# Half of the first early tile's matmuls moved among the last token tiles, with the order around them laid out anew

## The chip, the cores and the metric

The kernel runs on one core of one Trainium2 chip. The metric is the device time in microseconds of one execution. Three timed runs of the kernel before gave 883.22, 883.50 and 887.41 us (median 883.5).

## The reference, cut to what matters

```python
x = x + ffn(cond(x, cond_weights, itok), W_gate, b_gate, W_e, b_e)     # x: 64 x 64 x 1024, f32

cond:  W = weights[condition]                      # one 64 x 64 matrix of 16 for each batch entry
       y = einsum('bct,bcd->bdt', x, W)            # 4096 tokens of 1024 features
ffn:   logits = y @ W_gate + b_gate                # 8 experts
       _, top_idx = top_k(logits, 2)
       y_all = relu(einsum('bsd,edh->bseh', y, W_e) + b_e)
       out = mean of the two chosen experts' rows
```

So there are 8192 (token, expert) pairs, and each needs a row of 1024 times the expert's 1024 x 1024 matrix.

## The kernel before, in words

**Token stage.** The 4096 tokens are taken in 32 tiles of 128 (n = 0 to 31). For a tile, TensorE multiplies the tile of x by a block-diagonal matrix (`product`, L548) into one of two accumulators psO0 and psO1. ScalarE copies it to SBUF (`y_out`, L700) and writes it to `y_rows` in HBM (L703). VectorE transposes the copy (`turn_tokens`, L855). For every group g of four tiles there follows a chain that finds out which experts each token goes to: TensorE `gate` in two halves (L560), ScalarE copies the logits (L709), TensorE `unstack` (L580, L581), VectorE `choose` (L882 to L890), TensorE `ranks` (L587 to L593), VectorE `slots` (L895 to L928), TensorE `fill` (L572), VectorE `list_out` (L935 to L938). Then SyncE writes the lists to a table in HBM (`table_out`, L325). Dictionaries such as `GATE`, `RANKS` and `FILL` say after which tile each step stands on its engine. Product n+2 may not start before `y_out(n)`, because there are two accumulators.

**Split weights.** The expert product is done in three parts (high x high, low x high, high x low), so each chunk of 128 weight rows is split in two: ScalarE makes `w_hi`, VectorE the rest `w_lo`. Expert 0's eight chunks are split during the token stage (`split_first`).

**Early tiles.** Seven tiles of expert 0 (t = 0 to 6) need only the first entries of the table and are begun before the whole table is known. For each of them SyncE reads the list (`read_first`, L311), VectorE makes addresses (`read_from`, L972), GpSimd gathers the rows (L451), VectorE transposes them (`turn_early`, L1009), ScalarE takes the high part (`early_hi`, L730), VectorE the low part (`early_lo`, L1014), TensorE does 48 matmuls of 512 columns (`early_products`, L607: 8 chunks k, three parts, two halves of the columns), VectorE adds the bias (`finish_early`, L993), ScalarE applies relu (L724), and GpSimd adds the rows to the output. Steps of the last token groups stand between the matmuls of early tiles 0 and 1 as `hooks`.

**Main stage.** `schedule` (L942 to L966) works out which expert each tile has; the table is read back (ScalarE, L770) and turned into addresses (VectorE, L1081 to L1091). Then tile after tile is gathered (L465), transposed (L1020), split (L736, L1031), multiplied (L607), finished and added to the output. The weights of expert 1 and on are loaded by SyncE in chunks (L334) and split by ScalarE (L719) and VectorE (L875). With these inputs expert 0 has nine tiles (0 to 8), and tile 9 is the first of expert 1. 69 tiles are multiplied in all.

**What sets the order.** Each engine runs its program in the order written, and waits on semaphores. VectorE holds, in its order, `turn_rows(8)` and `finish_early(6)` behind the splitting of expert 1's first four chunks (`ahead(EARLY)`), and `early_lo(8)` behind those. SyncE's program goes, after the token tiles: stores and copies of x to the output (L305, L340; each `copy` is 1 MB and waits for the copy before the last), between them the last three `table_out`, then the rest of the copies, and only then the weights of expert 1:

```python
table_out(NG - 1)
read_first(6)
for c in range(6, len(left)):
    copy(c)
sp.wait_ge(s_alo, EARLY)
sp.wait_ge(s_bias, 16)
load_bias(1)
```

## Time and profile before

| what | value |
|---|---|
| timed runs | 883.22, 883.50, 887.41 us, median 883.5 |
| profiled execution, its own time | 886.42 us |
| its span (first to last instruction) | 884.7 us |
| mean granted TensorE clock | 0.984 |
| TensorE busy | 851.7 us (96%) |
| VectorE, ScalarE, GpSimd busy | 422.4, 256.5, 449.9 us |
| `L607` matmuls | 3 x 1104 records, 341.7 + 340.6 + 340.4 us |

The profiled execution took 886.42 us, 1.7 us more than its span, and 2.9 us more than the median of the timed runs. A record of the profile holds one of two levels of TensorE's clock: 1.0 stands for 2.4 GHz and 0.5 for 1.2 GHz, and a mean over a stretch lies between.

### The profile page before, as it was taken

The page shows a single profiled execution, that of the slowest core. Times are in us where ns is not written, and L with a number is a line of the kernel's source. Part 1 is how long each engine was busy: PE and PEld are TensorE (multiplying, and loading weights), DVE is VectorE, ACT ScalarE, POOL GpSimd, SP SyncE. Part 2 cuts the span into 40 slices and gives each one's busy share as a digit, 9 for nine tenths or more (in the row PEclk, how much of TensorE's full clock was granted, in tenths as well). Part 3 has the DMA queues.
Part 4 walks back from the last instruction along what each step waited for, and adds up shares of the span by engine and source line. Part 5 has one row for each costly group of instructions (what it writes and reads, how often), then busy time and mean ns, then how long its engine had stood idle before and what let it go on. Part 6 is the DMA issues. An engine that isn't in the chain of part 4 may idle for free.

```text
span 884.7 us, 16708 instructions
## 1 busy us (share of the span) xinstructions
PE 851.7 (96%) x4154; PEld 674.4 (76%) x4155; DVE 422.4 (48%) x595; ACT 256.5 (29%) x310; POOL 449.9 (51%) x500
## 2 busy tenths in 40 slices
PE   7898899999999999999999999999999999999993
PEld 4354478888888888888888888888888888888882
DVE  6697866836643273335533363336333733333320
ACT  5564512134421251114211331115111511112220
POOL 3002325366467667654665556555755565555311
PEclk9898999999999999999999999999999999999997
DMA  9999798998955695447754595547654664444433
GB/s 337 418 417 348 265 333 275 329 346 245 290 125 107 127 294 120 99 95 202 198 106 90 101 294 108 109 96 211 172 115 95 189 122 104 91 100 99 79 48 47
DMA packets 51034, 162.47 MB, mean 184 GB/s; under 512 B 11594, under 2 KB 11658, under 8 KB 50986
## 3 DMA queue, kind: packets, MB, share of 16 engines
q0 software_dynamic: 24544, 76.74, 40.3%
q1 hardware_dynamic: 20618, 67.79, 20.9%
q10 hardware_dynamic: 5840, 17.57, 5.1%
q8 instruction: 14, 0.23, 0.1%
q14 instruction: 18, 0.15, 0.0%
HBM read 106.74 MB, written 70.52 MB: 200 GB/s over the span
## 4 chain that ended last, share of the span: by engine, by line
PE 88%; DMA 4%; DVE 4%; issue 1%; ACT 1%; SPq 1%; POOL 0%; ACTq 0%; DVEq 0%; POOLq 0%
PE psO L607 85%; PE psO L548 2%; DMA y_rows<-ys 1%; DVE turned L855 1%; DMA first<-slot_table 1%; DMA slot_table<-lists 1%; DMA raw<-in_L_cond_weights 1%; ACT ys L700 1%; PE psG L560 1%; DVE w_lo L868 0%; SPq L325 0%; DVE place_hot L910 0%; DVE run_hot L918 0%; DVE idx_all L885 0%; POOL out L494 0%
## 5 line engine op out<-in xcount | busy, mean ns | idle before, releaser
L607 PE MATMUL psO<-w_hi,a_hi 128*128 (+1 forms) x1104 | 341.7, 391 | 0.2
L607 PE MATMUL psO<-w_lo,a_hi 128*128 (+1 forms) x1104 | 340.6, 390 | 0.0
L607 PE MATMUL psO<-w_hi,a_lo 128*128 (+1 forms) x1104 | 340.4, 389 | 0.0
L465 POOL DMA_INDIRECT rows<-y_rows,idx_g x248 | 260.6, 1051 | 106.7 <-issue 52.7
L607 PEld LDWEIGHTS psO<-w_hi,a_lo 128*128 128x128 f32 x1104 | 207.6, 188 | 43.3
L607 PEld LDWEIGHTS psO<-w_lo,a_hi 128*128 128x128 f32 x1104 | 207.7, 188 | 43.2
L607 PEld LDWEIGHTS psO<-w_hi,a_hi 128*128 128x128 f32 x1104 | 206.7, 188 | 44.4 <-issue 1.8
L1031 DVE TENSOR_TENSOR a_lo<-ys,a_hi 128x1024 fp32r<-128x1024 f32 x62 | 75.9, 1224 | 113.8 <-ACT a_hi L736 113.8
L724 ACT ACTIVATE ys<-ys 128x1024 f32<-128x1024 f32 x33 | 35.0, 1061 | 259.5 <-DVE ys L993 259.5
L724 ACT ACTIVATE rows<-rows 128x1024 f32<-128x1024 f32 x33 | 35.0, 1060 | 253.9 <-DVE rows L993 253.9
L993 DVE TENSOR_TENSOR ys<-psO,bias 128x1024 f32<-128x1024 f32 x33 | 40.3, 1222 | 125.4 <-PE psO L607 98.9
L993 DVE TENSOR_TENSOR rows<-psO,bias 128x1024 f32<-128x1024 f32 x33 | 40.4, 1225 | 119.2 <-PE psO L607 89.1
L875 DVE TENSOR_TENSOR w_lo<-raw,w_hi 128x1024 f32 x56 | 65.3, 1223 | 36.9 <-ACT w_hi L719 36.9
L1020 DVE STREAM_TRANSPOSE ys<-rows 128x1024 f32<-128x1024 f32 x62 | 76.8, 1238 | 9.6 <-DMA rows<-y_rows,idx_g 9.6
L494 POOL DMA_INDIRECT out<-rows,idx_s x31 | 55.9, 1802 | 39.9 <-issue 16.4
L494 POOL DMA_INDIRECT out<-ys,idx_s x31 | 52.1, 1682 | 38.6 <-ACT ys L724 17.7
L461 POOL COPY idx_g<-idx_all 128x4 uint32 x62 | 25.9, 418 | 86.9 <-issue 54.5
L736 ACT CAST a_hi<-ys 128x1024 fp32r<-128x1024 f32 x62 | 65.0, 1048 | 10.3 <-issue 10.2
L451 POOL DMA_INDIRECT raw<-y_rows,from_q x28 | 30.4, 1086 | 65.2 <-DVE bias L1009 35.1
L719 ACT CAST w_hi<-raw 128x1024 f32 x56 | 54.9, 1048 | 7.4 <-DMA raw<-in_L_ffn_W_e 6.2
L855 DVE STREAM_TRANSPOSE turned<-ys 128x1024 f32<-128x1024 f32 x32 | 39.5, 1240 | 14.5 <-ACT ys L700 12.4
L700 ACT COPY ys<-psO 128x1024 f32<-128x1024 f32 x32 | 32.4, 1012 | 23.1 <-PE psO L548 20.1
(141 smaller groups left out, 331.4 us busy)
## 6 DMA issues: line engine op xcount, KB each, us to landing
raw<-in_L_ffn_W_e SPq DMA_DIRECT2D x56, 512.0 KB, 6.0
y_rows<-ys ACTq DMA_DIRECT2D x32, 512.0 KB, 8.3
out<-in_x SPq DMA_DIRECT2D x14, 1024.0 KB, 9.7
rows<-in_x SPq DMA_DIRECT2D x16, 512.0 KB, 11.8
more_x<-in_x SPq DMA_DIRECT2D x16, 512.0 KB, 11.1
bias<-in_L_ffn_b_e SPq DMA_DIRECT2D x8, 512.0 KB
rows<-y_rows,idx_g POOLq DMA_INDIRECT x248
raw<-in_L_ffn_W_e POOLq DMA_DIRECT2D x4, 512.0 KB, 8.7
```

What stands on the lines that cost most here:

```text
L465: pool.indirect_dma_start(out=rows[:, slot, a * DQ:(a + 1) * DQ], out_offset=None, in_=y_parts[0:(1 + TOK) * Q, :], in_offset=bass.Indirec ...
L494: pool.indirect_dma_start(out=out, out_offset=bass.IndirectOffsetOnAxis(ap=idx_s[:, m:m + 1], axis=0), in_=o_sb[m], in_offset=None, comput ...
L607: last = nc.tensor.matmul(ps[:, h * BANK:(h + 1) * BANK], a[:, p, k * P:(k + 1) * P], w[:, bass.ds(slot + (k * H + h * BANK), BANK)], star ...
L700: nc.scalar.copy(ys[:, s, :].rearrange("p (q k j) -> p q k j", q=Q, k=KD), psO[n % 2][:, :].rearrange("p (k q j) -> p q k j", q=Q, k=KD)). ...
L719: nc.scalar.copy(w_hi[:, bass.ds(at, H)], raw[:, k, :]).then_inc(s_hi, 1)
L724: nc.scalar.activation(out_of(t), out_of(t), ACTF.Relu, scale=0.5).then_inc(s_out, 1)
L736: nc.scalar.copy(a_hi[:, m % 2, :], ys[:, m % 2, :]).then_inc(s_ahi, 1)
L855: V.transpose(turned[:, g % 2, :, s * R:(s + 1) * R], ys[:, s, :].rearrange("p (b i) -> p b i", i=R)).then_inc(s_turn, 1)
L875: V.tensor_tensor(w_lo[:, bass.ds(at, H)], raw[:, k, :], w_hi[:, bass.ds(at, H)], ALU.subtract).then_inc(s_split, 1)
L993: V.tensor_tensor(out_of(t), psO[m % 2][:, :], bias[:, bass.ds((e % 2) * H, H)], ALU.add).then_inc(s_bo, 1)
L1020: V.transpose(ys[:, p, :].rearrange("p (k a i) -> p k a i", k=KD, a=Q), rows[:, p, :].rearrange("p (a k j) -> p k a j", k=KD, a=Q)).then_i ...
L1031: V.tensor_tensor(a_lo[:, p, :], ys[:, p, :], a_hi[:, p, :], ALU.subtract).then_inc(s_alo, 1)
```

## The change: what it does

Early tile 0 no longer shares a buffer with the later ones: its transposed rows stand in a new buffer `early_f`. Its left 512 columns are multiplied in `psX`, a bank that is free by then (`ahead`, 24 matmuls), in six pieces behind token tiles 26 to 31. Its right 512 columns are multiplied in psO0 after the token tiles (`early_products(0, ..., hs=(1,))`). For that, `turn_early(0)` moves from behind tile 28 to behind tile 24, and ScalarE's `early_hi(0)` with it; `early_lo(0)` stands behind tile 25. Early tile 1 is turned behind tile 30 and tile 2 before `list_out(NG - 2)`. On VectorE, `choose` now stands ahead of `turn_tokens` and `read_from` behind it. The hooks are spread over early tiles 0, 1 and 2 in another order, and `fill(NG - 3)` has become one. In the middle stretch the table's addresses are made before `finish_early(3)`, `turn_early(5)` and `early_lo(5)`, and ScalarE issues the table's read before `early_hi(4)`.

```diff
@@ -106 @@
+            early_f = lend("early_f", [P, D])
@@ -250 @@
-        FILL = {G * g + 11: g for g in range(NG - 2)}
+        FILL = {G * g + 11: g for g in range(NG - 3)}
+        AHEAD = {26: [0], 27: [1, 2], 28: [3], 29: [4], 30: [5], 31: [6, 7]}
@@ products @@
-                                for h in range(NH):
+                                for h in hs:
                                     last = nc.tensor.matmul(
-                                        ps[:, h * BANK:(h + 1) * BANK], a[:, p, k * P:(k + 1) * P],
+                                        psX[:, :] if h in apart else ps[:, h * BANK:(h + 1) * BANK], a[:, p, k * P:(k + 1) * P],
...
+                def ahead(ks):
+                    if ks[0] == 0:
+                        pe.wait_ge(s_alo, 1)
+                        pe.wait_ge(s_split, RAW)
+                    products(tile(0, 0), None, 0, 0, ks, hs=(0,), apart=(0,))
...
+                    if n in AHEAD:
+                        ahead(AHEAD[n])
-                early_products(0, hooks={3: lambda: ranks(NG - 2), 4: lambda: gate(NG - 1, 1, 0),
-                                         5: lambda: gate(NG - 1, 1, 1), 7: lambda: unstack(NG - 1)})
-                early_products(1, hooks={0: lambda: fill(NG - 2), 2: lambda: ranks(NG - 1), 7: lambda: fill(NG - 1)})
-                early_products(2)
+                early_products(0, hooks={2: lambda: fill(NG - 3), 5: lambda: ranks(NG - 2),
+                                         7: lambda: gate(NG - 1, 1, 0)}, hs=(1,))
+                early_products(1, hooks={0: lambda: gate(NG - 1, 1, 1), 2: lambda: unstack(NG - 1),
+                                         5: lambda: fill(NG - 2), 7: lambda: ranks(NG - 1)})
+                early_products(2, hooks={4: lambda: fill(NG - 1)})
@@ scalar @@
-                    if n == NTILE - 4:
+                    if n == NTILE - 8:
                         early_hi(0)
-                early_hi(1)
+                    if n == NTILE - 2:
+                        early_hi(1)
                 logits_out(NG - 1)
...
-                early_hi(4)
-                relu(tile(0, 2))
                 for g in range(NG):
                     act.wait_ge(s_sc[g], LAND)
...
+                early_hi(4)
+                relu(tile(0, 2))
@@ vector, finish_early @@
-                    finish(tile(0, t), 0)
+                    if t:
+                        finish(tile(0, t), 0)
+                    else:
+                        dve.wait_ge(s_bias, 16)
+                        dve.wait_ge(s_mm, 1)
+                        own(V.tensor_tensor(o_first[:, 0, 0:BANK], psX[:, :], bias[:, 0:BANK], ALU.add))
+                        V.tensor_tensor(o_first[:, 0, BANK:H], psO[0][:, BANK:H], bias[:, BANK:H], ALU.add).then_inc(s_bo, 1)
@@ vector, the token tiles @@
-                    if n == NTILE - 3:
-                        early_lo(0)
-                    if n in FROM:
-                        read_from(FROM[n])
                     if n in UNSTACK:
                         choose(UNSTACK[n])
                     turn_tokens(n)
+                    if n in FROM:
+                        read_from(FROM[n])
+                    if n == NTILE - 7:
+                        early_lo(0)
...
-                    if n == NTILE - 4:
+                    if n == NTILE - 8:
                         turn_early(0)
+                    if n == NTILE - 2:
+                        turn_early(1)
+                    if n == NTILE - 1:
+                        early_lo(1)
                 list_out(NG - 3)
                 slots(NG - 2)
-                turn_early(1)
-                early_lo(1)
+                finish_early(0)
                 choose(NG - 1)
+                turn_early(2)
                 list_out(NG - 2)
-                finish_early(0)
+                early_lo(2)
                 slots(NG - 1)
                 read_from(4)
-                turn_early(2)
-                early_lo(2)
+                finish_early(1)
                 list_out(NG - 1)
-                finish_early(1)
...
                 schedule()
-                early_out(4, EARLY)
-                finish_early(3)
-                turn_early(5)
-                early_lo(5)
...
+                finish_early(3)
+                turn_early(5)
+                early_lo(5)
+                early_out(4, EARLY)
                 finish_early(4)
```

VectorE around token tiles 22 to 25. `turned<-ys` is `turn_tokens`, `from_q` is `read_from`, `w_lo` is `split_first`, `lists` is `list_out`, and `MAX` and `MAX_INDEX` are `choose`. Before:

```order
L855 STREAM_TRANSPOSE turned<-ys 128x32x32
L972 TENSOR_SCALAR from_q<-first,part_q 128x4
L882 MAX idx_all<-psR 128x8 x3
L883 MAX idx_all<-psR 128x8
L885 MAX_INDEX idx_all<-idx_all,psR 128x8 x3
L886 MAX_INDEX idx_all<-idx_all,psR 128x8
L887 TENSOR_TENSOR idx_all<-idx_all 128x64
L890 TENSOR_TENSOR mask<-idx_all 128x32
L855 STREAM_TRANSPOSE turned<-ys 128x32x32
L868 TENSOR_TENSOR w_lo<-bias,w_hi 128x1024
L855 STREAM_TRANSPOSE turned<-ys 128x32x32
L935 CAST lists<-psL 64x64
```

The same place in the changed kernel, from `choose` on, to the low part of early tile 0:

```order
L898 TENSOR_TENSOR idx_all<-idx_all 128x64
L901 TENSOR_TENSOR mask<-idx_all 128x32
L866 STREAM_TRANSPOSE turned<-ys 128x32x32
L983 TENSOR_SCALAR from_q<-first,part_q 128x4
L879 TENSOR_TENSOR w_lo<-bias,w_hi 128x1024
L866 STREAM_TRANSPOSE turned<-ys 128x32x32
L946 CAST lists<-psL 64x64
L1026 STREAM_TRANSPOSE early_f<-raw 128x1024
L866 STREAM_TRANSPOSE turned<-ys 128x32x32
L1031 TENSOR_TENSOR a_lo<-early_f,a_hi 128x1024
```

`from_q` has moved behind `choose` and the transpose, and the turn of early tile 0 and its low part stand on either side of tile 25's transpose. The same exchange of `from_q` and `choose` is made at tiles 19, 27 and 31.

TensorE from token tile 26 to tile 28. `psG` is `gate`, `psR` `unstack`, `psL` `fill`. Before:

```order
L548 MATMUL psO<-rows,raw 128x512 x2
L560 MATMUL psG<-turned,wgb 32x128 x16
L548 MATMUL psO<-rows,raw 128x512 x2
L580 MATMUL psR<-stack,LT 128x32
L581 MATMUL psR<-raw 128x32
L572 MATMUL psL<-place_hot,run_hot 64x64 x8
L548 MATMUL psO<-more_x,raw 128x512 x4
```

And in the changed kernel:

```order
L550 MATMUL psO<-rows,raw 128x512 x2
L562 MATMUL psG<-turned,wgb 32x128 x16
L609 MATMUL psX<-w_hi,a_hi 128x512
L609 MATMUL psX<-w_lo,a_hi 128x512
L609 MATMUL psX<-w_hi,a_lo 128x512
L550 MATMUL psO<-rows,raw 128x512 x2
L582 MATMUL psR<-stack,LT 128x32
L583 MATMUL psR<-raw 128x32
L574 MATMUL psL<-place_hot,run_hot 64x64 x8
```

The first chunk's three matmuls into `psX` stand between the gate of tile 26 and the product of tile 27, so whatever they wait for the product of tile 27 waits for too.

VectorE in the middle stretch, where the table becomes addresses (`idx_all`, `idx_row`). Before, the finish of tile 3 (`ys<-psO`), the turn and low part of tile 5 stand ahead of it:

```order
L987 SCALAR_TENSOR_TENSOR first_to<-first_f,behind 128x3
L993 TENSOR_TENSOR ys<-psO,bias 128x1024
L1009 STREAM_TRANSPOSE bias<-raw 128x1024
L1014 TENSOR_TENSOR a_lo<-bias,a_hi 128x1024
L1081 COPY ys<-ys 128x1024
L1083 STREAM_TRANSPOSE ys<-ys 128x8x4x32
L1085 TENSOR_SCALAR idx_all<-ys,part_q 128x1024
L1091 CAST ys<-ys 32x256 x4
```

And in the changed kernel:

```order
L1096 COPY ys<-ys 128x1024
L1098 STREAM_TRANSPOSE ys<-ys 128x8x4x32
L1100 TENSOR_SCALAR idx_all<-ys,part_q 128x1024
L1106 CAST ys<-ys 32x256 x4
L997 TENSOR_SCALAR ys<-ys,empty_to 128x256
L998 SCALAR_TENSOR_TENSOR idx_row<-ys 128x256
L1004 TENSOR_TENSOR ys<-psO,bias 128x1024
L1026 STREAM_TRANSPOSE bias<-raw 128x1024
L1031 TENSOR_TENSOR a_lo<-bias,a_hi 128x1024
```

The three instructions of early tiles 3 and 5 have moved behind the whole address block.

## Rows read from the trace of the kernel before

**Rows 1.** The page, busy time of each engine (share of the span) and instructions.

```profile
PE 851.7 (96%) x4154; PEld 674.4 (76%) x4155; DVE 422.4 (48%) x595; ACT 256.5 (29%) x310; POOL 449.9 (51%) x500
```

**Rows 2.** Windows: busy time of five engines, then granted clock, DMA share, GB/s.

```profile
75.00:85.00 10.00, 8.85 (x79) 4.71 (x76) 9.15 (x19) 2.20 (x6) 3.49 (x3) 0.66 0.83 308
...
110.00:120.00 10.00, 8.17 (x48) 6.21 (x52) 7.57 (x32) 0.00 (x0) 0.49 (x1) 0.83 1.02 389
...
140.00:200.00 60.00, 60.00 (x266) 49.66 (x265) 36.30 (x61) 14.77 (x14) 31.97 (x31) 1.00 1.02 328
```

**Rows 3.** Timeline, TensorE, tile 22: start, us, line, idle before it and releaser.

```profile
74.77 0.23 PE L587 MATMUL psR<-mask,raw 128*128 128x24 bf16 x3 [1.96 <-DVEq L891]
...
76.27 2.07 PE L560 MATMUL psG<-turned,wgb 128*32 128x128 f32 x32 [1.15 <-DVE turned L855]
78.27 3.78 PE L548 MATMUL psO<-more_x,raw 128*128 128x512 f32 x4
```

**Rows 4.** Timeline of TensorE, token tiles 26 to 31 and early tile 0.

```profile
90.57 1.98 PE L548 MATMUL psO<-rows,raw 128*128 128x512 f32 x4
...
93.49 1.98 PE L548 MATMUL psO<-rows,raw 128*128 128x512 f32 x4
...
106.97 1.96 PE L548 MATMUL psO<-more_x,raw 128*128 128x512 f32 x4 [0.92 <-ACT ys L700]
...
111.83 0.44 PE L572 MATMUL psL<-place_hot,run_hot 128*64 128x64 f16 x8 [2.00 <-DVEq L921]
...
117.11 0.62 PE L607 MATMUL psO<-w_lo,a_hi 128*128 128x512 f32 x2
117.56 0.61 PE L607 MATMUL psO<-w_hi,a_lo 128*128 128x512 f32 x2
```

**Rows 5.** Timeline of VectorE: read_from(0), tile 24, slots(4), tile 26, early tile 0.

```profile
72.69 0.23 DVE L972 TENSOR_SCALAR from_q<-first,part_q 128x4 uint32<-128x4 uint32 x1 [2.30 <-DMA first<-slot_table]
...
89.56 1.23 DVE L855 STREAM_TRANSPOSE turned<-ys 128x1024 f32<-128x1024 f32 x1
...
92.28 0.18 DVE L895 TENSOR_TENSOR idx_all<-idx_all,psR 128x64 f32<-128x64 f32 x1
...
96.21 1.25 DVE L855 STREAM_TRANSPOSE turned<-ys 128x1024 f32<-128x1024 f32 x1
...
103.59 1.25 DVE L1009 STREAM_TRANSPOSE bias<-raw 128x1024 f32<-128x1024 f32 x1 [0.21 <-DVE lists L938]
```

**Rows 6.** Timeline of ScalarE: high part of early tile 0.

```profile
104.87 1.04 ACT L730 CAST a_hi<-bias 128x1024 fp32r<-128x1024 f32 x1 [4.90 <-DVE bias L1009]
```

**Rows 7.** Timeline of VectorE: last list, schedule, then the address block.

```profile
139.86 0.21 DVE L938 TENSOR_TENSOR lists<-list_high,psL 64x64 uint32<-64x64 f32 x1
...
154.55 0.16 DVE L942 TENSOR_SCALAR raw<-raw 1x8 f32<-1x8 f32 x1
...
160.59 0.17 DVE L978 CAST parted<-first 128x12 f32<-128x12 uint32 x1
...
167.43 1.07 DVE L1081 COPY ys<-ys 128x1024 uint32<-128x1024 uint32 x1
...
173.34 0.47 DVE L987 SCALAR_TENSOR_TENSOR idx_row<-ys 128x256 uint32<-128x256 f32 x1
```

**Rows 8.** Timeline of GpSimd: the copy that opens the gather of tile 7.

```profile
172.23 0.32 POOL L461 COPY idx_g<-idx_all 128x4 uint32 x1 [6.19 <-issue]
```

**Rows 9.** Timeline of SyncE DMA issues: last eight copies, expert 1 weights.

```profile
147.79 29.81 SPq L340 DMA_DIRECT2D out<-in_x  x8
...
179.31 19.57 SPq L334 DMA_DIRECT2D raw<-in_L_ffn_W_e  x7
```

**Rows 10.** Timeline of VectorE: fourth split of expert 1, low part of tile 8.

```profile
198.97 1.23 DVE L875 TENSOR_TENSOR w_lo<-raw,w_hi 128x1024 f32 x1 [0.45 <-ACT w_hi L719]
...
204.53 1.23 DVE L1031 TENSOR_TENSOR a_lo<-ys,a_hi 128x1024 fp32r<-128x1024 f32 x1 [2.06 <-ACT a_hi L736]
```

**Rows 11.** The chain of waits where tile 8 starts: start, us, what.

```profile
206.17 0.08 issue
```

More of the change, by code:

```diff
@@ L594, in ranks, with products @@
                     last.then_inc(s_rank, 1)
-                def products(t, ps, e, slot, ks=range(KD), hooks={}):
+                def products(t, ps, e, slot, ks=range(KD), hooks={}, hs=range(NH), apart=()):
                     n, half, m = t
@@ L611, in products, with early_products @@
                                         stop=(k == KD - 1 and a is a_lo))
-                    if ks[-1] == KD - 1:
+                    if hs[-1] == NH - 1:
                         last.then_inc(s_mm, 1)
-                def early_products(t, ks=range(KD), hooks={}):
+                def early_products(t, hooks={}, hs=range(NH)):
+                    pe.wait_ge(s_alo, t + 1)
+                    if t >= 2:
+                        pe.wait_ge(s_bo, t - 1)
+                    else:
+                        pe.wait_ge(s_yc, NTILE - 1 + t)
+                    products(tile(0, t), psO[t % 2], 0, 0, hooks=hooks, hs=hs)
+                def ahead(ks):
                     if ks[0] == 0:
-                        pe.wait_ge(s_alo, t + 1)
+                        pe.wait_ge(s_alo, 1)
                         pe.wait_ge(s_split, RAW)
-                        if t >= 2:
-                            pe.wait_ge(s_bo, t - 1)
-                        else:
-                            pe.wait_ge(s_yc, NTILE - 1 + t)
-                    products(tile(0, t), psO[t % 2], 0, 0, ks, hooks)
+                    products(tile(0, 0), None, 0, 0, ks, hs=(0,), apart=(0,))
                 def all_products(t):
@@ L729, in early_hi @@
                         act.wait_ge(s_mm, t - 1)
-                    nc.scalar.copy(a_hi[:, t % 2, :], early_t).then_inc(s_ahi, 1)
+                    nc.scalar.copy(a_hi[:, t % 2, :], early_t if t else early_f[:, :]).then_inc(s_ahi, 1)
                 def parts(t):
@@ L1000, in finish_early @@
                         dve.wait_ge(s_yout[t % OS], 16 * NG)
-                    finish(tile(0, t), 0)
+                    if t:
+                        finish(tile(0, t), 0)
+                    else:
+                        dve.wait_ge(s_bias, 16)
+                        dve.wait_ge(s_mm, 1)
+                        own(V.tensor_tensor(o_first[:, 0, 0:BANK], psX[:, :], bias[:, 0:BANK], ALU.add))
+                        V.tensor_tensor(o_first[:, 0, BANK:H], psO[0][:, BANK:H], bias[:, BANK:H], ALU.add).then_inc(s_bo, 1)
                 def turn_early(t):
                     dve.wait_ge(s_yx[t % 2], (t // 2 + 1) * (Q * 16))
-                    if t:
+                    if t == 1:
+                        dve.wait_ge(s_split, KD)
+                    if t > 1:
                         dve.wait_ge(s_alo, t)
-                    else:
-                        dve.wait_ge(s_split, KD)
-                    V.transpose(early_t.rearrange("p (k a i) -> p k a i", k=KD, a=Q),
+                    V.transpose((early_t if t else early_f[:, :]).rearrange("p (k a i) -> p k a i", k=KD, a=Q),
                                 fetched[t % 2].rearrange("p (a k j) -> p k a j", k=KD, a=Q)).then_inc(s_zt, 1)
@@ L1013, in early_lo @@
                     dve.wait_ge(s_ahi, t + 1)
-                    V.tensor_tensor(a_lo[:, t % 2, :], early_t, a_hi[:, t % 2, :], ALU.subtract).then_inc(s_alo, 1)
+                    V.tensor_tensor(a_lo[:, t % 2, :], early_t if t else early_f[:, :], a_hi[:, t % 2, :], ALU.subtract).then_inc(s_alo, 1)
                 def turn_rows(t):
```

## The prediction

> **What bounds the kernel now.** The page says that TensorE is busy for 96% of the span [rows 1], and the chain of waits goes along its matmuls from 112 us to 871 us almost without a gap. Two matmul pairs of full clock start 0.455 us apart [rows 4], so one matmul costs 0.2275 us and a tile (48 of them) 10.92 us. The reader should take two things from this. Time can be won only where TensorE waits or runs at the low clock, which is before 112 us. And what is won there stays won only if nothing behind it comes due at a fixed time. So I read the timelines of the token stage first, then the DMA share of the stretch behind it, then the waits of tiles 2 to 8.
>
> In the token stage TensorE waits 1.96 us at tile 21 for `choose`, which stood on VectorE behind a `read_from` that waited 2.30 us for its list [rows 3, 5]. Then the work of tile 22 runs at about half speed. The windows give the length of the low clock: 0.34 / 0.5 x 10 us = 6.8 us in 75 to 85 us, and 0.17 / 0.5 x 10 = 3.4 us in 110 to 120 us [rows 2]. At half speed each costs half its length, 3.4 and 1.7 us. At the end TensorE waits 0.92 us for a copy and 2.00 us for `fill(5)` [rows 4].
>
> Behind it, the DMA engines are full: share 1.02 from 140 to 200 us [rows 2]. The last eight copies are issued over 29.81 us from 147.79, and expert 1's weights from 179.31 on [rows 9]. VectorE splits the fourth chunk at 198.97, and the low part of tile 8, which stands behind that, starts at 204.53 and lasts 1.23 [rows 10]. Tile 8 starts at 206.25, after a break of 0.08 us in the chain [rows 11]. So tile 8 has its operand 205.76, only 0.4 us before TensorE comes free. This is the second bound, and it hangs on the DMA queue, not on TensorE.
>
> **The change part by part.** All of it is a schedule by hand, from durations of rows.
>
> *`choose` ahead of `read_from` at tile 19.* Its wait for the list now stands behind the work that TensorE needs. `choose` (1.8 us: from behind `read_from` at 72.69 + 0.3 to `ranks` at 74.77) and the transpose (1.2, as of tile 24) begin at 70.4 us, when the transpose of tile 18 ends. TensorE's gate can start at 73.4 instead of 76.27, and tile 22's product at 74.4 instead of 78.27 [rows 3, 5]. With so short a wait I take the low clock there to be gone. VectorE becomes the limit for `fill(3)` (its `slots(3)`, 3.9 us as from 92.28 to 96.21, ends at 81.4 [rows 5]), and product 26 starts at about 86.7 instead of 90.57 [rows 4]: 3.9 us sooner.
>
> *`turn_early(0)` behind tile 24.* It starts when VectorE has done tile 24 and list 3. That was 91.1 us (89.56 + 1.17 + 0.39) and is now 88.6 [rows 5]. ScalarE has copied tile 24 from 83.5 on and is then held by `early_hi(0)`, which can start 1.28 us after the turn (104.87 against 103.59 before [rows 5, 6]), at 89.9. Copy 25 follows at 90.95, its transpose at 92.0, `early_lo(0)` at 93.2, and it lands at 94.4. TensorE stands at chunk 0 from 89.5: a wait of 4.9 us. Behind it is queued product 27, now at 95.1 instead of 93.49 [rows 4]. What tile 19 gave is spent, and 1.6 us more.
>
> *24 matmuls among tiles 26 to 31*: 24 x 0.2275 = 5.46 us. Beside them go the waits of 0.92 and of VectorE's transposes. Product 31 comes at 109.5 instead of 106.97, 2.5 us later [rows 4].
>
> *Behind tile 31.* `fill(5)` is no longer waited for (2.00 us), the low clock of 3.4 us need not come (1.7 us), and tile 0 has only 5.46 us left. Tile 1 starts at 121.4 instead of 111.83 + 0.37 + 10.92 + 1.7 + 3.8 of hooks = 128.6. That is 7.2 us, of which 1.1 us are hooks that still have to come. A wait of 0.4 us for the low part of tile 3 leaves 5.6 us at tile 3, on these sums 145.3 against 150.9.
>
> *The middle stretch.* The schedule takes 6.05 us (154.55 to 160.59) and the address block 6.6 (167.43 to 174.0) [rows 7]. Before, tile 5's turn stood between them. Now both stand ahead of it: VectorE comes to the schedule at 152.7 and to `finish_early(3)` at 165.3, the turn of tile 5 at 166.5, its low part lands at 170.0, and TensorE has finished tile 4 at 167.1. A new wait of 2.9 us is queued ahead of all of tile 5. It leaves 2.7 us at tile 7. In exchange the gather of tile 7, opened at 172.23 [rows 8], is opened at about 165, which nobody waits for.
>
> *Tile 8.* `list_out(6)` and the last list (139.86 before [rows 7]) come at 129.5 and 139.6, so SyncE's copies start when they did. Only the gap between the last copy (177.6) and the first weight load (179.31) can close, by up to 1.1 us, since tile 6's low part is ready 2 us sooner. Against that, the gathers of tiles 7 and 8 (1 MB) now stand among the copies in a full DMA stretch; before they stood beside the weight loads, so total bytes ahead of the fourth chunk are equal. I bound it by 1.1 us sooner and by 2.5 us later (a 1 MB copy takes 29.81 / 8 = 3.7 us, and the gathers move fewer bytes), and take 0.6 sooner, near the row's gap. The arrival of TensorE (203.5) no longer matters, and tile 8 starts at 205.6 instead of 206.25.
>
> The Trainium skill has a rule on this (DMA: Bandwidth & Descriptors, "Queues, rings and completion order"): each engine takes turns between the queues that have work, a packet at a time. By that rule the earlier gathers slow the copies on SyncE's queue and the weights start later, the upper bound. No row here separates the queues.
>
> *The sum.* On the profiled execution, 886.42 - 0.6 = 885.8. But it lies 2.9 us above the median of the runs shown, and the low clock at 112 us (1.7) is probably part of that difference: a median run has less for the change to take. And the wait of 4.9 us may bring low clock of its own: 3.4 us of it puts VectorE's lists and with them tile 8 later by 0.7, 6.8 us by 2.4 to 3.0. I take 1.1 for both. 883.5 - 0.6 + 1.1 = **884.0 us**, no change that can be told.
>
> **The rivals.** *A: the gain gets through.* If the DMA queue gives way when asked sooner, so that tile 8 follows TensorE's arrival, 2.7 us are left: 880.8. If tile 5's wait is not there either, 5.6 us: 877.9. For it: the gate before expert 1's weights (a semaphore of tile 6) comes 2 us sooner. Against: share 1.02 over 60 us [rows 2]. *B: the wait at tile 26 turns the clock down.* Before tile 22 TensorE had been idle for 1.96 and 1.15 us and the clock was low for 6.8 us [rows 2, 3]. A wait of 4.9 us is longer. Then products 27 to 29 run at half speed, every list comes 2.4 to 3.3 us later, the copies and the weights with them, and tile 8 too, 883.5 + 3 = 886.5. It goes over to slower by over 0.5% only together with C (2.5 us): 889. It decides when the low stretch starts before product 28. The Trainium skill says the same of waits inside a stream of matmuls (TensorE: Matmul & The Clock Gate, "HAM oscillation — how this bites in real kernels"); by that rule the clock does fall at tile 27. *C: the earlier gathers push the weights back* by up to 2.5 us, with the clock as it was: 886. For it: full DMA; against: equal bytes. *D: the change does not do what it says*: the matmuls ahead only move waits, because VectorE is the limit, and tile 1 starts near 126. The sums put it at 121.4; and since tile 8 is bound elsewhere, D ends at the forecast's time too.
>
> **How the numbers follow.** Forecast 0.50; A 0.20, of which half reaches the larger gain; B 0.17; C 0.13, and of B and C together a third lies with both. This kernel can tell 0.5% (4.4 us) from no change. Faster than 879.1: 0.10, with 0.01 for what I don't see. Slower than 887.9: 0.10, same reason. The range that should hold 8 in 10 goes from A's first value, 880.5, to B with a part of C, 888.
>
> **What would show it.** Right: product 22 near 74.4 at full clock; a TensorE wait of 4 to 5 us ahead of the first `psX` matmul; tile 1 some 7 us sooner; a wait of 2 to 3 us at tile 5; copies and weight loads at the same times as before, and a wait of 1 to 2 us at tile 8 for its low part. Wrong: expert 1's weights issued before 176 us, no wait at tile 5, or tile 8 started before 203; or the last list later than 142 us.

## The result, and the profile after

| what | before | changed |
|---|---|---|
| timed runs, same chip | 885.45 us median (883.22 to 890.86, 4 runs) | 895.03 us median (894.86 to 896.33, 4 runs) |
| ratio to before | | 1.0101, 95% interval 1.0081 to 1.0121 |
| profiled execution, its span | 886.42, 884.7 us | 895.16, 893.4 us |
| mean granted TensorE clock | 0.984 | 0.985 |

The change made the kernel slower by 1%, 9.6 us. The forecast was 884.0 us, and the range ended at 888.

The page of the changed kernel, its first section, against [rows 1]:

```profile
PE 852.7 (95%) x4154; PEld 674.2 (75%) x4155; DVE 422.5 (47%) x596; ACT 256.7 (29%) x310; POOL 447.1 (50%) x500
```

TensorE is busy for 1 us more in a span 8.7 us longer. The mean clock is the same. So the loss is mostly waiting. The windows say where, with the columns of [rows 2]:

```profile
75.00:85.00 10.00, 8.56 (x56) 4.15 (x56) 8.82 (x32) 4.69 (x10) 3.88 (x4) 0.86 1.02 371
...
110.00:120.00 10.00, 9.79 (x58) 6.96 (x59) 7.72 (x26) 3.24 (x4) 1.70 (x2) 1.00 0.79 280
140.00:200.00 60.00, 52.43 (x227) 42.04 (x226) 34.59 (x66) 10.44 (x10) 29.22 (x29) 0.94 0.92 295
```

From 140 to 200 us TensorE was busy without a break before; now 7.6 us of it are empty, its clock is 0.94, and the DMA share fell from 1.02 to 0.92. The token stage is better than before: at a higher clock from 75 us on (0.86 for 0.66), and with less idle time from 110 us on. The timeline of TensorE: its places that answer to [rows 3, 4], the last `fill`, and every wait over 1 us behind token tile 31:

```profile
74.78 1.98 PE L550 MATMUL psO<-more_x,raw 128*128 128x512 f32 x4
...
88.68 1.98 PE L550 MATMUL psO<-rows,raw 128*128 128x512 f32 x4
...
94.42 0.50 PE L609 MATMUL psX<-w_hi,a_hi 128*128 128x512 f32 x1 [1.19 <-DVE a_lo L1031]
...
95.22 1.88 PE L550 MATMUL psO<-rows,raw 128*128 128x512 f32 x4
...
111.42 1.88 PE L550 MATMUL psO<-more_x,raw 128*128 128x512 f32 x4
...
124.96 0.73 PE L609 MATMUL psO<-w_hi,a_hi 128*128 128x512 f32 x2
...
139.22 0.73 PE L609 MATMUL psO<-w_hi,a_hi 128*128 128x512 f32 x2 [1.46 <-DVE a_lo L1031]
...
144.88 0.44 PE L574 MATMUL psL<-place_hot,run_hot 128*64 128x64 f16 x8
...
151.26 0.73 PE L609 MATMUL psO<-w_hi,a_hi 128*128 128x512 f32 x2 [0.28 <-DVE a_lo L1031]
...
180.90 1.22 PE L609 MATMUL psO<-w_hi,a_hi 128*128 128x512 f32 x2 [6.92 <-DVE a_lo L1031]
```

The rows are products 22, 26, 27 and 31, and the starts of early tiles 1, 2, 3 and 5. Tile 1 starts 3.8 us sooner than before (128.77). Tile 3 starts when it did (151.61): 1.46 us went at tile 2, and more of the hooks stand behind tile 1's start. Tile 5 waits 6.92 us, and starts at 180.90 instead of 173.37; its first matmuls take 1.22 us a pair instead of 0.73, the lower clock of 1.2 GHz. Tile 8 follows at 215.39 instead of 206.25, without a wait. So in this trace the loss is made at tile 5: 7.5 us of later start, and 1.85 us of low clock behind it (tile 6 begins at 193.63, 12.73 us after tile 5, where a tile takes 10.88 at full clock). Nothing is gained or lost after tile 8 beyond half a microsecond.

The chain of waits of the changed kernel shows what stood ahead of tile 5. It is followed back to the end of the token stage (start, us, what), with most of its pieces left out:

```profile
118.69 13.57 DMA bias<-in_L_ffn_b_e
132.46 0.70 DVE more_x L1017
...
135.58 1.26 DVE bias L1026
136.86 1.06 ACT a_hi L740
137.94 1.23 DVE a_lo L1031
...
153.27 4.47 DMA slot_table<-lists
...
159.85 9.63 DMA ys<-slot_table
169.51 1.09 DVE ys L1096
...
177.25 1.25 DVE bias L1026
178.51 1.05 ACT a_hi L740
179.59 1.27 DVE a_lo L1031
180.90 34.20 PE psO L609 x142
```

At its head stands a transfer that the prediction never named: the 512 KB load of the bias, issued behind the stores and the first copies. VectorE's timeline shows who waits for it, the last list, which answers to [rows 7], and the wait for the high part of early tile 4:

```profile
132.46 0.69 DVE L1017 TENSOR_TENSOR more_x<-psX,bias 128x512 f32<-128x512 f32 x1 [8.84 <-DMA bias<-in_L_ffn_b_e]
...
133.79 0.31 DVE L893 MAX8 idx_all<-psR 128x8 f32<-128x8 f32 x3
...
145.36 0.22 DVE L948 TENSOR_SCALAR list_high<-psL 64x64 f32<-64x64 f32 x1 [0.97 <-issue]
145.61 0.21 DVE L949 TENSOR_TENSOR lists<-list_high,psL 64x64 uint32<-64x64 f32 x1
...
161.52 1.23 DVE L1031 TENSOR_TENSOR a_lo<-bias,a_hi 128x1024 fp32r<-128x1024 f32 x1 [4.82 <-ACT a_hi L740]
```

L1017 is `finish_early(0)`. It waits 8.84 us, and the last `choose` (the MAX8 row), the turn of tile 2, the list of group 6, `slots` and the last list stand behind it. The last list comes at 145.61 instead of 139.86; just before it VectorE idles for 0.97 us, until the `fill` that TensorE starts at 144.88 has made its input. SyncE follows, against [rows 9] (expert 0's bias, the last table, eight copies, expert 1's bias and weights):

```profile
118.69 0.62 SPq L331 DMA_DIRECT2D bias<-in_L_ffn_b_e  x1
...
146.77 6.78 SPq L327 DMA_DIRECT2D slot_table<-lists  x8
...
155.35 31.83 SPq L342 DMA_DIRECT2D out<-in_x  x8
187.28 0.76 SPq L331 DMA_DIRECT2D bias<-in_L_ffn_b_e  x1
188.15 47.31 SPq L336 DMA_DIRECT2D raw<-in_L_ffn_W_e  x16
```

Copies and weights are 7.6 and 8.8 us late. Of the 7.6 us, 5.75 are the list; the eight issues of the last table took 6.78 us where they took 3.56 before.

### The profile page after: what moved, and what is told of

Same layout as the page of the kernel before. It is cut to its first block, busy times and chain, and to the rows that moved or that the text cites. A ratio compares the mean times of both kernels' runs of the same rounds, so it can differ in the third digit from the quotient of the medians.

```text
span 893.4 us, 16710 instructions
## 1 busy us (share of the span) xinstructions
PE 852.7 (95%) x4154; PEld 674.2 (75%) x4155; DVE 422.5 (47%) x596; ACT 256.7 (29%) x310; POOL 447.1 (50%) x500
## 4 chain that ended last, share of the span: by engine, by line
PE 79%; DMA 8%; SPq 4%; issue 3%; DVE 2%; ACT 1%; ACTq 0%; POOL 0%; DVEq 0%; POOLq 0%
PE psO L609 78%; DMA y_rows<-ys 3%; DMA slot_table<-lists 2%; SPq L327 2%; DMA bias<-in_L_ffn_b_e 2%; DMA ys<-slot_table 1%; SPq L313 1%; ACT ys L710 1%; SPq L324 1%; PE psO L550 1%; DMA raw<-in_L_cond_weights 1%; DVE bias L1026 0%; DVE a_lo L1031 0%; SPq L342 0%; SPq L303 0%
## 5 line engine op out<-in xcount | busy, mean ns | idle before, releaser
L453 POOL DMA_INDIRECT raw<-y_rows,from_q x28 | 28.2, 1008 | 75.9 <-DVEq L984 53.2
```

## The experiments

Each ratio is to the kernel before, run beside it on the same chip, with its 95% interval. The experiments ran on several chips, where before had medians of 885.5 to 886.0 us. Three dots mark what is left out of a diff or a timeline.

**1. The bias loaded sooner** (changed kernel, `e1_bias_soon`).

```diff
                 for n in range(NTILE):
+                    if n == NTILE - G:
+                        sp.wait_ge(s_split, KD)
+                        load_bias(0)
...
-                sp.wait_ge(s_split, KD)
-                load_bias(0)
                 table_out(NG - 3)
```

> The changed kernel with one DMA moved: the bias of expert 0 is issued on SyncE behind tile 27's steps instead of behind the copies and the filler rows. Theory 1 (the finish of early tile 0, which the change put ahead of choose(7), slots(7) and the turn of tile 2, waits 8.8 us for the bias; the last list, the copies, the weights and tile 5 follow): the wait goes, the last list comes near 139.6 us instead of 145.6, tile 5 waits some 3 us instead of 6.9, and the time falls by 7 to 9 us, to within 1.5 us of the kernel before. Theory 2 (the loss is the middle order, the address block ahead of tile 5): the time falls by 2 us at most. Theory 3 (the loss comes from matmuls into a second bank and the longer token stage): no change.

Measured: 890.03 us (889.15 to 892.25), ratio 1.0053 (1.0033 to 1.0073). That is 5.0 us less than the changed kernel by the medians and 4.3 by the ratios, and less than the 7 to 9 us expected. The finish no longer waits and the last list comes at 141.66. Its timeline of VectorE (the finish), of TensorE (the first `psX` matmul, tile 5) and of SyncE:

```profile
122.52 0.69 DVE L1018 TENSOR_TENSOR more_x<-psX,bias 128x512 f32<-128x512 f32 x1
```

```profile
93.80 0.50 PE L610 MATMUL psX<-w_hi,a_hi 128*128 128x512 f32 x1 [4.41 <-DVE a_lo L1032]
...
173.81 1.22 PE L610 MATMUL psO<-w_hi,a_hi 128*128 128x512 f32 x2 [4.41 <-DVE a_lo L1032]
```

```profile
182.59 46.88 SPq L336 DMA_DIRECT2D raw<-in_L_ffn_W_e  x16
```

So about half of the loss goes with the wait for the bias. With it gone, the two waits that the prediction named stand there at 4.41 us each.

**2. The middle stretch as before** (changed kernel, `e2_old_middle`): VectorE makes the address block behind `finish_early(3)`, `turn_early(5)` and `early_lo(5)` again.

```diff
+                early_out(4, EARLY)
+                finish_early(3)
+                turn_early(5)
+                early_lo(5)
...
-                finish_early(3)
-                turn_early(5)
-                early_lo(5)
-                early_out(4, EARLY)
                 finish_early(4)
```

> The changed kernel with VectorE's middle stretch in the order of before (tile 3's finish, tile 5's turn and low part ahead of the address block). Theory 1: the wait for the bias stays, the last list stays at 145 to 146 us, tile 5's wait of 6.9 us shrinks to under 2, but expert 1's weights are issued near 188 us all the same and tile 8 now waits for its low part: the time falls by 1 to 3 us only. Theory 2: it falls by 6 us or more. Theory 3: no change.

Measured: 893.35 us (891.06 to 894.40), ratio 1.0085 (1.0065 to 1.0105), 1.7 us less than the changed kernel, as theory 1 had it. The wait at tile 5 is gone and tile 8 waits instead, for its low part behind expert 1's weights:

```profile
209.48 1.22 PE L609 MATMUL psO<-w_hi,a_hi 128*128 x2 [4.79 <-DVE a_lo L1048]
```

**3. Both** (`e3_both`, edits 1 and 2).

> Both edits of the two kernels before in one. Theory 1 with the second bound (weights of expert 1 behind the copies in a full DMA stretch): TensorE waits for nothing up to tile 8, arrives there near 200 us and waits some 4 to 5 us, since the weights come as before: the time equals the first kernel's within 1 us, that is about 1 us below the kernel before. If there is no second bound (rival A of the prediction): 5 us below the kernel before.

Measured: 893.72 us (888.74 to 894.66, 7 runs), ratio 1.0074 (1.0048 to 1.0100). The two edits do not add up. Tile 8 waits 6.04 us, and the clock turns down behind it (mean 0.74 from 200 to 220 us). The expected sum of gains failed: taking out the wait at tile 5 only brings TensorE sooner to weights issued at 182.58.

**4. Only `choose` first** (kernel before, `e4_choose_first`).

```diff
-                    if n in FROM:
-                        read_from(FROM[n])
                     if n in UNSTACK:
                         choose(UNSTACK[n])
                     turn_tokens(n)
+                    if n in FROM:
+                        read_from(FROM[n])
```

> The kernel before with one part of the change alone: on VectorE, choose ahead of the transpose and read_from behind it, at tiles 19, 23, 27 and 31. By the timelines product 22 starts near 74.4 us instead of 78.3 and the low clock of 6.8 us at 76 us goes; the last list comes 2 to 3 us sooner (136.6), so do the copies and the weights, and tile 8 starts 2 to 3 us sooner: 2.5 us below the kernel before, at least 1. If VectorE takes all of it back: no change.

Measured: 884.27 us (882.45 to 888.53, 12 runs), ratio 0.9992 (0.9977 to 1.0007). The profiled execution has no low clock at tile 22 and expert 1's weights at 176.14 instead of 179.31, but the median is that of before within what can be told. The gain of at least 1 us that was expected isn't shown.

**5. Expert 1's weights ahead of the last copies** (`e3_both` with this, `e5_weights_first`).

```diff
-                for c in range(6, len(left)):
+                for c in range(6, len(left) - 4):
                     copy(c)
+                sp.wait_ge(s_sched, 1)
+                sp.wait_ge(s_bd, NTILE * PAIR)
+                load_chunk(1, 2)
+                load_chunk(1, 3)
+                for c in range(len(left) - 4, len(left) - 2):
+                    copy(c)
+                sp.wait_ge(s_zt, EARLY)
+                load_chunk(1, 0)
+                load_chunk(1, 1)
+                for c in range(len(left) - 2, len(left)):
                     copy(c)
...
-                sp.wait_ge(s_zt, EARLY)
-                sp.wait_ge(s_sched, 1)
-                sp.wait_ge(s_bd, NTILE * PAIR)
-                for k in range(KD):
-                    if k >= RAW:
-                        sp.wait_ge(s_split, KD + k - RAW + 1)
+                for k in range(RAW, KD):
+                    sp.wait_ge(s_split, KD + k - RAW + 1)
                     load_chunk(1, k)
```

> e3_both with SyncE's last copies and expert 1's weights exchanged: chunks 2 and 3 ahead of the last four copies, chunks 0 and 1 ahead of the last two. e3's trace shows a wait of 6.04 us at tile 8 and a low clock behind it. Theory 1 (tile 8's low part hangs on weights that stand behind the copies in a full DMA stretch): the fourth split comes some 3 us or more sooner than e3's 202.8, the wait at tile 8 falls below 3 us, and the time falls by 4 to 7 us from e3's 893.7, to 887 to 890. Rival (the wait at tile 8 comes from VectorE's or ScalarE's order): no change.

Measured: 889.74 us (883.37 to 895.51, 12 runs), ratio 1.0026 (1.0001 to 1.0050). Tile 8 no longer waits, so its wait did come from the weights. But tile 10 waits 2.77 us for its low part, which stands on VectorE behind four splits of later weight chunks (219.95 to 228.12 us), and tile 12 waits 1.12 us for its own, whose gathered rows VectorE got only at 247.78, after a wait of 8.12 us. What is moved ahead in the full DMA stretch seems to push something else back; no run separates this from the order on the engines.

**6. Early tile 0's high part one tile later, the matmuls from tile 28 on** (`e3_both` with this, `e6_high_later`).

```diff
-        AHEAD = {26: [0], 27: [1, 2], 28: [3], 29: [4], 30: [5], 31: [6, 7]}
+        AHEAD = {28: [0, 1], 29: [2, 3], 30: [4, 5], 31: [6, 7]}
...
-                    if n == NTILE - 8:
+                    if n == NTILE - 7:
                         early_hi(0)
...
-                    if n == NTILE - 7:
+                    if n == NTILE - 6:
                         early_lo(0)
```

> e3_both with the high part of early tile 0 behind copy 25 instead of copy 24 on ScalarE, its low part behind tile 26 on VectorE, and the 24 matmuls ahead behind tiles 28 to 31, two chunks each. Theory (the 4.4 us that TensorE waits at the first chunk, and the low clock of 6.8 us behind it, come from ScalarE being held by a turn that VectorE reaches late): the wait and the low clock go, product 31 starts 3 us sooner and the last list comes 3 to 4 us sooner than in e3. Tile 8 is still bound by the weights, which move with the lists: 3 to 4 us below e3, 889 to 891. If the wait only moves: no change from e3.

Measured: 891.02 us (888.13 to 892.17), ratio 1.0052 (1.0038 to 1.0066), against 1.0074 of `e3_both`; the intervals overlap. The wait at the first `psX` matmul is gone, with 2.34 us at the next `unstack` in its place. Tile 8 still waits 4.90 us. Against `e3_both` the medians are 2.7 us apart and the time is at the end of the expected range (889 to 891).

**7. The kernel before with the bias late** (`e7_bias_late`): the load behind `copy(2)` and `copy(3)`.

```diff
-                sp.wait_ge(s_split, KD)
-                load_bias(0)
                 table_out(NG - 3)
                 read_first(4)
                 copy(2)
                 copy(3)
+                sp.wait_ge(s_split, KD)
+                load_bias(0)
```

> The kernel before with the load of expert 0's bias issued behind the third and fourth copies, about 12 us later than it was. Theory 1 (a finish of early tile 0 that waits for the bias costs what the wait is long, because slots(7), the last list, the copies and the weights stand behind it): the bias lands near 137 us, the finish waits 6 to 8 us, the last list comes 5 to 8 us later, and the time rises by 5 to 9 us. Rival (only the new order is hurt by such a wait, the old one has slack): under 1.5 us.

Measured: 892.27 us (890.11 to 895.95), ratio 1.0059 (1.0044 to 1.0074), 6.3 us over the 886.0 of before, with none of the change in it. On VectorE the finish of early tile 0 waits, and `slots(NG - 1)` stands behind it; on TensorE the last `fill` then waits for that:

```profile
138.41 1.22 DVE L993 TENSOR_TENSOR more_x<-psO,bias 128x1024 f32<-128x1024 f32 x1 [9.46 <-DMA bias<-in_L_ffn_b_e]
```

```profile
143.11 0.64 PE L572 MATMUL psL<-place_hot,run_hot 128*64 128x64 f16 x8 [4.56 <-DVEq L921]
```

The bias is issued 12.8 us later (126.94), the last list comes at 147.34 and expert 1's weights at 188.40, as late as in the changed kernel. Behind the wait of 4.56 us the clock was low as well (0.74 from 135 to 150 us).

**8. Edits 1, 2, 5 and 6 together** (`e8_both_later`).

> e6_high_later and e5_weights_first in one: no wait in the token stage and the weights ahead of the last copies. Theory: TensorE arrives at tile 8 near 199 to 201 us with a wait under 4 us, so tile 8 starts 2 to 4 us sooner than the 206.2 of the kernel before: 881 to 884, below the kernel before (885.5). Rival (the DMA stretch is full, so the order of its transfers does not matter): as e6, 889 or more.

Measured: 887.76 us (883.57 to 891.07, 12 runs), ratio 1.0022 (1.0005 to 1.0038): the best with the matmuls ahead, still not below before, and not the 881 to 884 expected. Tile 12 waits 3.77 us. In before its low part was ready at 249.76 us, 0.4 us before it started.

**9. The finish put back** (changed kernel, `e9_finish_back`).

```diff
                 slots(NG - 2)
-                finish_early(0)
                 choose(NG - 1)
                 turn_early(2)
                 list_out(NG - 2)
+                finish_early(0)
                 early_lo(2)
```

> The changed kernel with one line moved: VectorE's finish of early tile 0, with its wait for the bias, stands behind the list of group 6 and ahead of the low part of early tile 2, instead of ahead of the last choose. The bias load stays where it is. Theory (that finish is what held the last lists): the lists no longer wait for the bias, the last list comes near 143 instead of 145.6 us, SyncE's copies and the weights of expert 1 come 2 to 3 us sooner, and the time is 891.5 to 893 against 895.0. Only a part comes back, since the bias still lands at about 132 and then holds the low part of early tile 2 and so the start of that tile. Rival (the loss of the changed kernel is in the matmuls ahead and their wait, the bias wait only lies beside it): the last list comes sooner, but the time stays within 1 us of 895.

Measured: 889.39 us (888.18 to 895.98, 10 runs), ratio 1.0058 (1.0034 to 1.0082). One line moved gives 5.6 us back by the medians and 3.8 by the ratios, more than expected; the rival (within 1 us of 895) is out. The spread is wide: seven of the ten runs took 888.2 to 889.8 us and three 893.95 to 895.98, which is next to the changed kernel's 894.9 to 896.3. VectorE (last choose, finish, last list), then TensorE (first `psX` matmul, tiles 2, 3, 5), then SyncE's issues of the last table:

```profile
128.77 0.32 DVE L893 MAX8 idx_all<-psR 128x8 f32<-128x8 f32 x3 [3.88 <-PE psR L583]
...
134.07 0.69 DVE L1017 TENSOR_TENSOR more_x<-psX,bias 128x512 f32<-128x512 f32 x1 [0.24 <-DVE lists L949]
...
144.99 0.22 DVE L948 TENSOR_SCALAR list_high<-psL 64x64 f32<-64x64 f32 x1 [0.99 <-PE psL L574]
145.24 0.21 DVE L949 TENSOR_TENSOR lists<-list_high,psL 64x64 uint32<-64x64 f32 x1
```

```profile
95.62 0.79 PE L609 MATMUL psX<-w_hi,a_hi 128*128 128x512 f32 x1 [4.41 <-DVE a_lo L1031]
...
138.83 0.72 PE L609 MATMUL psO<-w_hi,a_hi 128*128 128x512 f32 x2 [0.87 <-DVE a_lo L1031]
...
150.97 0.74 PE L609 MATMUL psO<-w_hi,a_hi 128*128 128x512 f32 x2 [0.35 <-DVE a_lo L1031]
...
175.15 1.01 PE L609 MATMUL psO<-w_hi,a_hi 128*128 128x512 f32 x2 [2.09 <-DVE a_lo L1031]
```

```profile
146.40 3.56 SPq L327 DMA_DIRECT2D slot_table<-lists  x8
```

`choose` now comes 5.0 us sooner (128.77 for 133.79), and the list of group 6 3.3 us (133.62 for 136.96), but the last list only 0.4 us. It waits in both traces for the last `fill`, which stands on TensorE within early tile 2. Tile 2 starts at 138.83 here and at 139.22 in the changed kernel, since its low part stands behind the finish in both, and since this execution lost time at `psX` to the wait of 4.41 us with a low clock, which that of the changed kernel had not. What got faster is the table behind the list: its eight issues took 3.56 us and not 6.78, its read was issued at 152.51 and not at 157.99, the address block starts at 163.68 and not at 169.51, and tile 5 starts 5.75 us sooner. In the changed kernel two 1 MB copies are issued at 144.10, just ahead of the table; here they go at 140.17, since the list of group 6 is sooner. That these copies are what slows the table is an argument from one trace of each kernel, and not shown.

**10. Kernel before with `choose` first and the weights first** (`e10_choose_weights`, edits 4 and 5, no matmuls ahead).

> The kernel before with two edits: choose and the turn ahead of the read of the list (as in the run with that alone, 884.3), and the weights of expert 1 issued ahead of the last copies. It has none of the matmuls ahead. Theory (tile 8 is held by the weights behind the copies, so that taking them forward lets the sooner lists through, and without the matmuls ahead there is no 4.4 us wait and no low clock from it): 881 to 884, no wait at tile 8. Rival (the third bound, operands of tiles 10 to 12 behind the full DMA stretch, takes it all back, as in the two runs with the weights first so far): tile 12 starts at about 250 us as before, with a wait of 1 to 4 us there, and the time is 884 to 888.

Measured: 885.08 us (883.52 to 889.14, 12 runs), ratio 1.0000 (0.9985 to 1.0014). TensorE has no wait from 111.3 us to the end, so neither tile 8 nor tile 12 holds it, and the rival is out as well. The theory's picture is right and its gain (881 to 884 us) is not there: with both bounds out of the way, the kernel is held by TensorE itself and the token stage. Its chain of waits, the last piece but the closing ones:

```profile
138.38 730.79 PE psO L614 x3222
```

**11. ScalarE's high part of tile 4 ahead of the table again** (`e9_finish_back` with this, `e11_high_four`).

```diff
+                early_hi(4)
+                relu(tile(0, 2))
                 for g in range(NG):
                     act.wait_ge(s_sc[g], LAND)
...
-                early_hi(4)
-                relu(tile(0, 2))
```

> The kernel with VectorE's finish of early tile 0 put back (889.4 us), and one more edit undone: ScalarE takes the high part of early tile 4 and the relu of tile 2 ahead of the wait for the table again, and not behind it. Theory: in that kernel the low part of early tile 4 waited 1.95 us on VectorE for that high part, and the schedule and the address block stood behind it; without the wait the schedule starts about 2 us sooner (155.3 instead of 157.3), and the block starts when the table has come back, at 161.7 to 162.5 instead of 163.68. So tile 5 waits 0 to 1 us instead of 2.09, the low clock behind it goes, and the time falls by 1.5 to 3 us, to 886.5 to 888; the rest up to the kernel before is the wait of 4.41 us at the first psX matmul with its low clock. Rival (the block is held by the read of the table, not by the order on ScalarE): the block starts near 163.7 all the same, and the time stays within 1 us of 889.4.

Measured: 891.39 us (889.59 to 900.40, 11 runs), ratio 1.0070 (1.0045 to 1.0095). The theory fell. The schedule did start 1 us sooner, but the block waited for the table to come back:

```profile
164.27 1.08 DVE L1096 COPY ys<-ys 128x1024 uint32<-128x1024 uint32 x1 [1.65 <-DMA ys<-slot_table]
```

Tile 5 waited 2.76 us. Neither the theory's 886.5 to 888 came nor the rival's time within 1 us of 889.4, though the rival named what holds the block. The 4.82 us that VectorE waited for that high part in the changed kernel lay beside the write and the read of the table.

**12. The same with the bias sooner** (`e12_all_holds`, edits 1, 9 and 11).

> The same, and the bias loaded sooner as well (ahead of the store at token tile 28), so that all three holds on VectorE behind the token tiles are gone: the finish of early tile 0, its bias, and the high part of early tile 4. What is left of the changed kernel is the matmuls ahead with their wait, and the address block ahead of early tile 5. Theory: the last list comes near 141.5, tile 5 waits under 2 us, and tile 8 then comes up against expert 1's weights; 886 to 888, so no better than the run without the sooner bias by more than 1 us, and still slower than before by about the wait of 4.41 us and its low clock less the matmuls saved. Rival (the bias still cost something after the finish was moved, since the low part of early tile 2 stood behind it): under 886.

Measured: 890.83 us (889.92 to 892.78, 7 runs), ratio 1.0053 (1.0034 to 1.0073). Neither came out. It isn't under 886, and not below edit 11 by more than can be told, so no further cost of the bias shows once the finish is moved. And it isn't at 886 to 888. The last list came at 144.29, 2.6 us later than in edit 1: TensorE was 1.45 us later at `fill(5)` (116.97 for 115.52), with more low clock behind `psX`, and tile 2 waited 0.87 us for a low part that stands behind the finish, where it waited for nothing in edit 1. And the table took 11 us to come back:

```profile
154.09 11.01 DMA ys<-slot_table
```

## Why the prediction was wrong

**The step that failed.** The prediction says: "`list_out(6)` and the last list (139.86 before [rows 7]) come at 129.5 and 139.6, so SyncE's copies start when they did". They came at 136.96 and 145.61, and the copies 7.6 us late. The prediction summed VectorE's instructions in their new order and left out what one of them waits for. `finish_early(0)` moved from behind `list_out(NG - 2)` to ahead of `choose(NG - 1)`, and it waits for the bias. In the kernel before, SyncE's timeline has the load and VectorE's the finish:

```profile
114.10 1.62 SPq L329 DMA_DIRECT2D bias<-in_L_ffn_b_e  x1
```

```profile
129.59 1.23 DVE L993 TENSOR_TENSOR more_x<-psO,bias 128x1024 f32<-128x1024 f32 x1 [0.25 <-DVE lists L938]
```

There it was covered. In the new place the finish was due at 123.6 (132.46 less the wait of 8.84). The bias was issued 4.6 us later besides (118.69). On SyncE it stands behind the table of group 4, whose list came 2.1 us later (105.27 for 103.16) and whose eight issues took 5.44 us instead of 3.54. It landed at 132.3. That the wait costs time is shown from three sides: by moving its cause (edit 1, 890.0), by moving the waiting instruction (edit 9, 889.4), and by making the load late in the kernel before (edit 7, 6.3 us more without any of the change). The text did name the sign to look for, a last list later than 142 us, but gave it no price.

**What the wait does not explain.** The last list missed its forecast by 6.0 us, and in the traces of the changed kernel and of edits 1, 9 and 12 it waits for the last `fill`, which the new hooks put within early tile 2 on TensorE. Tile 1 came at 124.96 and not at 121.4, which is 3.6 us; tile 2 then waited 1.46 us for its low part, the one that stands behind the bias; 1.0 us is left. So the last list would have come near 144.2 without the wait for the bias, 4.3 us later than before. Even in edit 1, with no such wait, it comes at 141.66. The sum for tile 1 is a second step that failed. The other way from the bias to the time goes over the list of group 6, 7.5 us behind its forecast, and the slow table, as edit 9 tells it.

**Token stage: right in mechanism.** Product 22 came at 74.78 (74.4 forecast), the first `psX` matmul at 94.42 (94.4), product 27 at 95.22 (95.1). Product 26 came at 88.68 and not at 86.7, and product 31 at 111.42 and not at 109.5: a stretch of low clock remained, 0.14 / 0.5 x 10 = 2.8 us of it between 75 and 85 us. Tile 1 came at 124.96 and not at 121.4, 1.9 us of it from product 31 and 1.6 from the stretch behind it, where the gate for the last group stood still for 0.75 us.

**Rival B came true in the experiments, and not in the trace of the changed kernel.** In seven experiments the first `psX` matmul waited 4.41 us. The windows of 90 to 105 us read 0.89 in one of them and 0.77 in the other six, which is 3.3 and 6.9 us at 1.2 GHz, for 24 matmuls that take 5.46 us in all. In the changed kernel's own profile the matmul waited 1.19 us behind a gate that had waited twice, and the clock stayed up. The Trainium skill says that waits inside a stream of matmuls turn the clock down (TensorE: Matmul & The Clock Gate, "HAM oscillation — how this bites in real kernels"); these seven traces agree. Edit 6, which takes this wait away, gives 2.7 us against `e3_both` (the intervals overlap), and edit 10, which has neither the matmuls ahead nor the new order behind them, lies 2.7 us under edit 8 (2.0 by the ratios, whose intervals overlap too). So the matmuls ahead brought no gain in any arrangement tried.

**The middle stretch: right in kind, too small.** A wait of 2.9 us at tile 5 was forecast. It was 6.92 us with the late lists, 4.41 us with the bias sooner, 2.09 us with the finish put back. It hangs on the last list and on the read of the table (9.6 us in the changed kernel, 11.0 in edit 12). The prediction let the address block follow the schedule at once and had no term for that read. The low clock behind it (pairs of 1.22 us) was not in the sum.

**Tile 8: right in kind, too small.** The "second bound" is real, though larger than the 1 to 2 us forecast: as soon as TensorE is not held at tile 5, tile 8 waits 4.8 to 6.0 us for expert 1's weights (edits 2, 3, 6). In the changed kernel itself it did not show, because tile 5 had already taken more. Behind it lies a third bound that the prediction missed, the low parts of tiles 10 and 12 (edits 5, 8).

**Where the 9.6 us stand.** The two edits that take the wait for the bias off the last `choose` give back 5.0 and 5.6 us by the medians, 4.3 and 3.8 by the ratios; that is shown. The other 4 to 5 us are in part the low clock behind tile 5: with edit 1 tile 5 starts at 173.81, only 0.4 us later than before, and tile 8 at 209.40, 3.2 us later than before, because the first 6 us or so behind the wait ran at the low clock (pairs 0.85 us apart instead of 0.455), which cost 2.9 us. How much of the rest is the order of the middle stretch and how much the later token stage is not settled: removing one wait brings up the next, so the parts do not add.

**A slip in the text.** The lower end of the range, 880.5, is called A's first value, which stands there as 880.8. Nothing hangs on it.

## What to carry to other kernels

When an instruction is moved forward on its engine, list every semaphore that it waits for, with the time at which each is released, and not only its duration. A load that was always in time becomes a wait for everything queued behind its reader. When a step is moved on one engine, look also at which engine makes its input: here the last list hung on a `fill` that had been moved into a later tile. And where several bounds lie within 5 us of one another, a gain ahead of the first was gone by the last in every arrangement tried, while a loss came through in large part (a wait of 9.46 us cost 6.3 in edit 7).

## What was not expected of the hardware

A 512 KB load took 13.57 us to land in the busy stretch behind the token tiles. The last piece of the same read of the table took 9.6 and 11.0 us to come back in the two kernels where it lay on the chain of waits. The last table is 2 KB a piece in eight pieces; issuing them took 6.78 us in the changed kernel and 3.56 in edit 9.

A wait of TensorE of the same length does not always have the same effect. That of 4.41 us was followed by 3.3 us of low clock in one kernel and by 6.9 us in six. The wait of 2.00 us ahead of `fill(5)` was followed by about 3.3 us of it in before and in edits 4 and 10, and by none in edit 7 (1.00 from 105 to 120 us).
